# Moving the normalisation of one more group of attention probabilities from VectorE to GpSimd

## The reference, cut to what matters

```
def _layer(x, wqkv, qs, ksc, wo, lg, lb, w1, b1, w2, b2):
    h = shift_token(x)
    q, k, v = jnp.split(h @ wqkv, 3, axis=-1)          # then into heads
    q = l2norm(q) * qs
    k = l2norm(k) * ksc
    q, k = rotary_xpos(q, k)
    o = local_attention(q, k, v)                       # softmax over own and previous window
    x = x + o @ wo
    h = shift_token(x)
    mu = h.mean(-1, keepdims=True)
    var = h.var(-1, keepdims=True)
    h = (h - mu) / jnp.sqrt(var + 1e-05) * lg + lb
    a, g = jnp.split(h @ w1 + b1, 2, axis=-1)
    return x + (a * jax.nn.gelu(g, approximate=False)) @ w2 + b2
...
    sim = jnp.where(mask, -jnp.finfo(sim.dtype).max, sim)
    attn = jax.nn.softmax(sim, axis=-1)
    out = jnp.einsum('bhwij,bhwjd->bhwid', attn, bv)
```

## Time and profile before

| | |
|---|---|
| timed runs, median (lowest to highest) | 862.38 us (861.84 to 864.74) |
| the profiled execution | 866.81 us |
| its span, first to last instruction | 865.1 us |
| mean granted TensorE clock | 0.930 of full speed |
| normalising products on POOL (L848) | 32, 1039 ns each |
| normalising products on DVE (L2085) | 32, 699 ns each |

### The profile page before, as it was taken

One profiled execution on the slowest core, in us unless ns is written; L12 is line 12 of the kernel. 1 busy time (PEld: TensorE's weight loads), 2 busy tenths in 40 slices (PEclk: granted clock), 3 DMA queues, 4 the chain that ended last, 5 costly groups with the idle time before them and its releaser, 6 DMA issues. The chain is left out here.

```text
span 865.1 us, 23912 instructions
## 1 busy us (share of the span) xinstructions
PE 718.2 (83%) x7870; PEld 531.2 (61%) x7870; DVE 675.1 (78%) x2051; ACT 585.2 (68%) x1750; POOL 522.5 (60%) x603
## 2 busy tenths in 40 slices
PE   5989999999989842994554578999999999999675
PEld 3667666666759832983443245666666666667464
DVE  5778888888876856563576589999999999998474
ACT  3678889888870011773343277899999999999551
POOL 4645555555552684334872498888888888884621
PEclk9999999999999965998698789999999999999898
DMA  8464444444410092332110000000000000000000
GB/s 216 124 218 167 166 166 170 173 172 173 171 57 2 25 325 89 104 114 65 44 37 0 1 1 2 2 2 2 3 2 2 2 3 2 2 2 2 1 26 25
DMA packets 62021, 61.87 MB, mean 72 GB/s; under 512 B 13275, under 2 KB 50766, under 8 KB 61774
## 3 DMA queue, kind: packets, MB, share of 16 engines
q1 hardware_dynamic: 59854, 56.17, 19.8%
q0 software_dynamic: 2048, 4.20, 1.6%
HBM read 17.55 MB, written 23.00 MB: 47 GB/s over the span
## 5 line engine op out<-in xcount | busy, mean ns | idle before, releaser
L687 POOL TENSOR_TENSOR scratch<-scratch 128x256 f32<-128x256 f32 (+1 forms) x128 | 105.9, 827 | 112.6 <-DVE scratch L1720 112.5
L1075 ACT ACTIVATE scratch<-psum,scratch 128x128 f32<-128x128 f32 x256 | 114.9, 479 | 8.5 <-DVE scratch L2073 8.2
L923 ACT ACTIVATE scratch<-psum,scratch 128x256 f32<-128x256 f32 x256 | 117.6, 480 | 3.6 <-DVE scratch L1738 3.6
L827 POOL TENSOR_TENSOR scratch<-scratch,mhalf 128x16 f32<-128x16 f32 x32 | 93.5, 2923 | 0.0
L817 POOL TENSOR_TENSOR big<-big 128x512 f32<-128x512 f32 x64 | 81.6, 1275 | 6.3 <-DVE big L2047 6.1
L1191 PE MATMUL psum<-scratch 128*64 128x256 f32 x480 | 62.8, 383 | 2.2 <-DMA scratch<-xT 2.2
L1731 DVE TENSOR_TENSOR psum<-psum,causal 128x512 f32<-128x512 f32 x64 | 44.8, 699 | 20.4 <-PE psum L1215 20.1
L1215 PE MATMUL psum<-scratch 64*128 64x128 f32 (+1 forms) x512 | 59.3, 350 | 0.0
L1075 ACT ACTIVATION_READ_ACCUMULATOR scratch<-psum,scratch 128x1 f32 x256 | 57.6, 225 | 0.0
L1241 PE MATMUL psum<-scratch 128*64 128x256 f32 (+1 forms) x512 | 55.7, 338 | 2.2 <-DVE scratch L1726 2.2
L923 ACT ACTIVATION_READ_ACCUMULATOR scratch<-psum,scratch 128x1 f32 x256 | 54.7, 214 | 0.0
(11 more groups left out here) (291 smaller groups left out, 2179.8 us busy)
## 6 DMA issues: line engine op xcount, KB each, us to landing
routed_in<-zfill SPq DMA_DIRECT2D x64, 256.0 KB, 2.1
scratch<-w_qkv SPq DMA_DIRECT2D x60, 193.0 KB, 2.2
scratch<-xT SPq DMA_DIRECT2D x60, 128.0 KB, 2.1
scratch<-routed_in SPq DMA_DIRECT2D x47, 64.0 KB, 1.8
routed_out<-scratch SPq DMA_DIRECT2D x23, 128.0 KB, 1.8
big<-in_L_ffn_W SPq DMA_DIRECT2D x1, 2048.0 KB, 8.9
stream<-in_L_attn_resid_pre SPq DMA_DIRECT2D x4, 256.0 KB, 3.6
big<-in_L_ffn_b SPq DMA_DIRECT2D x1, 1024.0 KB, 11.7
```

Source lines behind the costliest of these rows:

```text
L687: pool.tensor_tensor(y, y, rs[s][:, t, :].unsqueeze(2).to_broadcast([P, 2, n]), ALU.mult).then_inc(b_p, 1)
L827: pool.tensor_tensor(o, ss[:, :, j * H1:(j + 1) * H1], half, ALU.pow).then_inc((f_rq, f_rk)[j], 1)
L923: last = act.activation(pr[s][:, t, h, :], scores_of(s)[:, h, t * S:(t + 1) * S], ACT.Exp, bias=nb[s][:, 2 * t + h:2 * t + h + 1], accum_o ...
L1075: last = act.activation(p1[a][:, h, t, :], bank(SCORES[a][h])[:, t * P:(t + 1) * P], ACT.Exp, bias=nb1[a][:, h, t:t + 1], scale=rq8[m % 2] ...
```

## The change

Group 2 goes from DVE to POOL. DVE now takes only the reciprocal for it, and the product is called on POOL directly behind `ln_rstd(n - 3)`. The counts of the semaphores follow: `f_r` and `f_pp` now rise three times in a unit, in the order of groups 1, 3, 2, and `f_p` once.

```diff
--- before.py
+++ after.py
@@ -401,6 +401,7 @@
         OUT_BANK, SHIFT_BANK, NORMED_BANK, FFN_BANK = 5, 2, 4, 6
         HIDDEN = ((1, 0), (3, 7))
         RANK = (1, 0, 3, 2)
+        BY_POOL = (1, 3, 2)
 
         def scores_both(a):
 
@@ -844,7 +845,7 @@
             def normalise1(m, a):
                 if not live(m):
                     return
-                pool.wait_ge(f_r, m * 2 + a // 2 + 1)
+                pool.wait_ge(f_r, m * 3 + BY_POOL.index(a) + 1)
                 pool.tensor_tensor(p1[a], p1[a], rs1[a].unsqueeze(3).to_broadcast([P, 2, TB, P]),
                                    ALU.mult).then_inc(f_pp, 1)
 
@@ -869,6 +870,7 @@
                 scale_keys(n - 1)
                 normalise1(n - 2, 3)
                 ln_rstd(n - 3)
+                normalise1(n - 2, 2)
                 add_rot(n, 0)
                 inverse_norm(n - 1, 0)
                 add_rot(n, 1)
@@ -1532,8 +1534,9 @@
             def turn_probs1(m, half_):
                 if not live(m):
                     return
-                pe.wait_ge(f_p, m * 2 + half_ + 1)
-                pe.wait_ge(f_pp, m * 2 + half_ + 1)
+                if half_ == 0:
+                    pe.wait_ge(f_p, m + 1)
+                pe.wait_ge(f_pp, m * 3 + 2 * half_ + 1)
                 if half_ == 0:
                     freed(pe, (f_gl, m - 1, m - 2), summed(m - 1, 0), turned(m, 1))
                     freed(pe, rotated(m + 2, 1), (f_x, m - 2 + B, m - 3), turned(m, 1))
@@ -2077,7 +2080,7 @@
                 if not live(m):
                     return
                 dve.wait_ge(f_e, m * 4 + RANK[a] + 1)
-                if a % 2:
+                if a in BY_POOL:
                     dve.reciprocal(rs1[a][:], sm1[a][:]).then_inc(f_r, 1)
                     return
                 dve.reciprocal(rs1[a][:], sm1[a][:])
```

## The result

The changed kernel took 877.61 us (median of 4 runs, 875.7 to 880.5) against 863.13 us before (4 runs, 861.84 to 864.74): a ratio of 1.0164, 95% interval 1.0135 to 1.0194, so 14.5 us or 1.6% slower. The forecast was 876.3 us. The profiled execution of the changed kernel took 875.7 us (span 873.7).

A forecast was written before the change was run, and what follows sets the result against it. It took three loops as equally tight: DVE, PE with ACT, and POOL's row holding DVE's small instructions. 12 steps x 0.99 = 11.9 us plus 2.0 at the ends gave 862.4 + 13.9 = 876.3 us, range 865 to 881.

The forecast's parts named there:

- Three loops: Per step of 20.86 us: DVE's own work, PE with ACT, and POOL's row from power L842 to the third addition.
- The norm: DVE's L2134 instructions: held by POOL's new product and first addition, ending about 0.35 us later though DVE was 0.5 ahead.
- L2064: DVE scaling of 128x16 numbers: arrives at 6.51 inside POOL's second addition (5.78 to 7.04) and waits to 7.07.
- The two maxima: DVE's L2073 products: first waits for POOL's copy to 8.38, second for the third addition to 10.23, 0.99 us later.
- the sign: DVE's first-maximum L2073: about 0.56 us expected; 0.16 us again would mean the forecast is wrong and the first rival holds.
- the first rival: DVE wins a close race, second maximum not held; only the norm's delay on PE remains: 864 to 868 us, chance 0.12.
- The sum: Whole kernel: 12 steps x 0.99 = 11.9 us plus 2.0 at the ends, together +13.9 us, giving 876.3 us.
- The term of the ends: Pipeline filling and emptying, 4 of 16 units: the product costs between 0 and 4.2 us, 2.0 taken as the middle.
- What was cost at nothing: Group 2's reciprocal staying on DVE, and PE's second half of transposes waiting for POOL's product, covered by 0.43 us: 0 us.

The follow-up runs named there:

- the extra product: The kernel before plus one more 128x512 product on POOL behind the power, on a tile nobody reads or waits for: 880.59 us, ratio 1.0175.
- the extra power: The kernel before plus one more power of 128x4 numbers on POOL, in the place of an added product: 879.69 us, ratio 1.0174.

## Why the prediction was right

- **The bound.** Three loops were named as equally tight. The runs show POOL's as one of them: without DVE's product the step stayed at 20.86 us, and a microsecond more on POOL behind the power cost 0.99 to 1.01 us whichever instruction it was. That over PE and ACT shows in the 0.41 us for which DVE waited when only POOL's row was shortened. POOL's row was read as without a gap; it has 0.25 us of idle time before the copy of `copy_x` (L808, now L809), the same in both kernels, so the 0.99 us is not touched by it.
- **The norm.** Forecast: gate at 0.16, first instruction at 1.34 waiting to 1.72, third at 1.95 waiting to 2.99. Measured from the power: gate at 0.19, first instruction from 1.37 to 1.76, third from 1.94 to 2.99.
- **L2064** (L2067 now): forecast to arrive at 6.51 and end at 7.07; it came at 6.50 and ended at 7.08.
- **The two maxima: one step was wrong in its detail.** The forecast had the second scaling (L2068) get through between the addition and the copy, and the first maximum's product be held by L862. In the trace L2068 was held by L860, which had begun 0.01 us before it, and ended at 7.63; the first maximum's product then came at 8.29 and was free, 0.16 us. So the sign that the text had named for the first rival appeared, and the first rival didn't hold: the standing still had only moved one instruction forward. Had L2068 got through at 7.00, the first maximum's product would have come at about 7.83 (0.83 later, the forecast's own distance), inside L862 (7.72 to 8.33), and been held there. Either way DVE reaches the second maximum's product after the third addition has begun (forecast at 9.06, measured at 9.13), and leaves it at 10.23, as forecast. The mistake in the text was to take one instruction of the row for the sign, where only the last of them, which does hold DVE, tells.
- **The sum.** Per step 0.99 was forecast; measured over 12 steps 11.62 / 12 = 0.97 (0.99 in the first eleven, 0.72 in the last, which runs into the emptying of the pipeline). The term of the ends, taken as +2.0, is less sure. In the profiled executions the stretch from the block's first copy to the first power grew by 1.1 us (from 473.50 to 534.55 before, from 470.66 to 532.84 after), and the stretch behind the thirteenth power shrank by 1.3 us (865.1 - 784.83 against 873.7 - 794.74), -0.2 together: the profiles thus explain 11.4 us. The medians differ by 14.5, with an interval of 11.7 to 16.7 us, which leaves 2.9 beside the steps. The profiles can't decide it: the profiled execution of before was 3.7 us above its median, that of after 1.9 below, and the stretch behind the thirteenth power lasted 82.2 us with the extra product and 78.3 with the extra power, though both cost the same per step. So the 11.6 us of the steps are explained; that the whole came within 1.3 us of the forecast also took some luck with the ends.
- **What was cost at nothing.** PE's second half of transposes didn't wait for the late product: its 32 transposes stand in one piece, and what L1494 then waited for is the norm (L2137). L1494 started 3.39 us behind the power, forecast 3.40.

```profile
665.51 1.21 PE L1550 MATMUL psum<-ident,scratch 64*128 64x64 f32 x32
667.39 1.22 PE L1494 MATMUL psum<-ident,big 64*128 64x64 f32 x32 [0.68 <-DVE scratch L2137]
```

## What to carry to other kernels

A busy share near 100% can be standing still: look for one instruction with two durations (0.16 and 1.10 us), and see whether its long ones end with an instruction of the other engine. When work is moved to an engine with idle time, what decides is not how much idle time it has but what stands behind the new instruction in its list, and who is held until that is done. Put the work into the gap itself; moving it ahead of the power that closed the gap took the loss from 1.6% to 0.3%, and taking an addition out of the row behind the power as well made the kernel 0.7% faster than before.

## What the runs showed of the hardware

- A POOL product, addition or copy holds DVE's small products of two SBUF tiles and its scalings of SBUF tiles until its end (0.16 against 1.10 us, 0.30 against 1.05 us). Not every DVE instruction that reads SBUF is held: in the kernel before, a reduction of 128x32 numbers (the row below) took 0.18 us inside an addition (664.54 to 665.80). A POOL power holds none of them: beside 2.90 us of L828 the norm's instructions took 0.30 us, and a product of 128x4 numbers 0.16 us (662.62, above). The Trainium skill ("SBUF — State Buffer", section "Who interferes with whom") says that whoever issues first gets the shared ports for the whole instruction and the other blocks; the held products agree with it (1.10 us, where POOL was first), the powers do not (0.30 us), and here the measurement decides. That it is ports that hold DVE is the page's explanation; the runs show only who stands still, and until when.

```profile
665.20 0.18 DVE L2055 TENSOR_REDUCE scratch<-scratch 128x16 f32<-128x32 f32 x1
```

- Where two instructions reach the same point within 0.01 us (L2068 and L860, 671.00 and 670.99), the later one can be held for the whole of the other; in an earlier step of the kernel before the same pair of instructions (L2065 and L859) began both at 519.35, and DVE went through with 0.16 us:

```profile
519.35 0.63 POOL L859 COPY big<-big 64x512 f32<-64x512 f32 x1
```
